# VectorE's side stages moved from the end of a step to the middle of it, in a graph-attention kernel on one core

## The chip, the cores and the metric

The kernel runs on 1 core of a Trainium2 chip. The metric is the time of the kernel on the device in microseconds (us), here the median of 3 runs. Engines: TensorE (PE in the profile) multiplies matrices, VectorE (DVE), ScalarE (ACT) and GpSimd (POOL) work elementwise, SyncE (SP) starts DMAs. Each engine has one queue of instructions, taken in order, and they wait for each other on semaphores.

## The reference, cut to what matters

x has 4096 rows of 128 numbers, adj is 4096 by 4096; there are 8 heads of 16.

```python
qkv = layer_norm(x, g1, be1) @ w_qkv
q, k, v = ...                                       # 8 heads of 16
scores = jnp.einsum('nhd,mhd->hnm', q, k) * SCALE
scores = jnp.where((adj != 0)[None, :, :], scores, -jnp.inf)
attn = jax.nn.softmax(scores, axis=-1)
out = jnp.einsum('hnm,mhd->nhd', attn, v).reshape(n, DIM)
x = x + out @ w_proj + b_proj
h2 = layer_norm(x, g2, be2)
return x + jax.nn.gelu(h2 @ w1 + b1) @ w2 + b2
```

## The kernel before

**Tiles and steps.** After a first stage (keys, values, the first masks) the queries are worked off in 8 tiles of 512 rows, i = 0 to 7; a short last pass, i = 8, finishes tile 7. Each tile has STEPS = 64 steps g: 4 pairs of heads, 16 steps for each. A step has two blocks n = 0 and 1 of 128 keys. `made_by(i)` gives three flags: b (there is a next tile), c (a tile is being made), d (there is a tile before, whose output is being finished).

**What TensorE does in a step** (`body`, from line 941): `scores(g, 0)`; a stage for ScalarE if there is one (`act_fill`); `weigh_values` of step g - 3 (L879, probabilities times values); `scores(g, 1)`; a stage for VectorE if there is one (`dve_fill`). `scores` holds the two score matmuls of the block (L964, L966), in banks of 4 that ScalarE empties with exp (L614, two exps a step), and after each of them one `row` (L815). Two matmuls (L976) add the mask; where `pool_masked` holds, in block 1 of the odd steps g for the most part (28 of the 64 steps), they are left out, and GpSimd masks the probabilities instead. Such a block is called whole below.

**The rows.** They run ahead, for the next pair of heads or tile: each of a step's UNITS = 4 rows is a 128 by 512 tile of scores of which VectorE takes the masked maximum (`row_maximum`, L652). r0 and r1 stand in block 0, r2 and r3 in block 1. Row tiles and VectorE's side stages go through one ring of three PSUM banks, `ring_ps`. The order in it is written out by hand: `ROW_PLACE` and `DVE_PLACE` number its places, and TensorE writes a place only when VectorE has taken all up to the one three places before (`place - 3`). A place that a tile doesn't use (tile 0 has no stages for a tile before) still counts as a place.

**VectorE's side stages** (`DVE_FILLS`, line 71): "sums" at steps 4, 20, 36, 52 (TensorE L912, then a reciprocal L749), "back" at steps 5, 21, 37, 53 (L918, then a multiplication L752), "proj" at step 7 (L925, then an addition L756 and the layer norm's statistics L298 to L306), "down" at steps 23 and 25 (L935 and L937, then an addition L763). The sums and back of steps 20 to 53 belong to the tile being made (flag c), all others to the tile before (flag d).

**ScalarE's side stages** (`ACT_FILLS`, line 67) stand after block 0; "shift" is at steps 4, 20, 36 and 52 among others, "q" at 24, 27, 33, 40. After step 21 ScalarE makes the gelu (L620), whose result "down" reads; after step 9 it makes a square root (L625) for which VectorE waits at step 10.

Of the kernel before, what the change touches and what calls it, by code (L numbers as in the profile page):

```python
# [25 lines left out]
CHUNKS = N // 512  # L26
# [31 lines left out]
UNITS = 4  # L58
# [12 lines left out]
DVE_FILLS = {4: ("sums", PAIRS - 1), 5: ("back", PAIRS - 1), 7: ("proj",), 23: ("down", 0), 25: ("down", 1)}  # L71
# [30 lines left out]
def fills_of(table, b, c, d):  # L102
    on = {"b": b, "c": c, "d": d}
    return {g: w for g, w in table.items() if on[made_for(w)]}
# [3 lines left out]
SCORE_PLACE, ACT_PLACE, ROW_PLACE, DVE_PLACE = {}, {}, {}, {}  # L108
for _g in range(STEPS):
    for _b in range(BLOCKS):  # L110
        SCORE_PLACE[_g, _b] = len(SCORE_PLACE) + len(ACT_PLACE)
        if _b == 0 and _g in ACT_FILLS:
            ACT_PLACE[_g] = len(SCORE_PLACE) + len(ACT_PLACE)
    for _x in range(UNITS):
        ROW_PLACE[_g, _x] = len(ROW_PLACE) + len(DVE_PLACE)
    if _g in DVE_FILLS:
        DVE_PLACE[_g] = len(ROW_PLACE) + len(DVE_PLACE)
SCORE_PLACES = len(SCORE_PLACE) + len(ACT_PLACE)
ROW_PLACES = len(ROW_PLACE) + len(DVE_PLACE)
assert SCORE_PLACES % 2 == 0 and ROW_PLACES % 3 == 0 and FIRST_UNITS % 3 == 0  # L120
# [2 lines left out]
def row_steps(b, c):  # L123
    return STEPS if b else (STEPS - AHEAD if c else 0)
# [35 lines left out]
def pool_masked(p, m):  # L160

    return m % 4 == 3 and not (p == 2 and m % 8 == 7)
# [22 lines left out]
def row_unit(g, x):  # L185

    u = UNITS * (g + AHEAD) + x
    ahead, u = divmod(u, TILE_UNITS)
    p, u = divmod(u, QUARTER_UNITS)
    j, u = divmod(u, 2 * CHUNKS)  # L190
    return ahead, p, j, u // 2, 1 - u % 2
# [7 lines left out]
def program(nc, x, adj, w_qkv, w_proj, b_proj, w1, b1, w2, b2, g1, be1, g2, be2, const, out):  # L199
    with ExitStack() as ctx:  # L200
# [115 lines left out]
        def neg_max_order(i, p, jj):  # L316

            return i * (PAIRS * 2) + (p * 2 + jj)

        def made(ring, i, bcd, place):  # L320

            return ring.before(i) + ring.upto(bcd, place)
# [313 lines left out]
        def _(dve):  # L636
# [20 lines left out]
            def negated_maxima(n, jj, taken):  # L657

                if not (isinstance(n, int) and n < 2):
                    dve.wait_ge(split_step, SPLIT_OPS * (n - 1))  # L660
                dve.wait_ge(row_taken, taken)
                nc.vector.tensor_reduce(neg_max[:, jj, :], row_max[:, 2 * jj:2 * jj + 2, :, :], AX.X, ALU.max,  # L662
                                        negate=True).then_inc(neg_max_done, 1)
# [51 lines left out]
            for st in range(FIRST_STEPS):  # L715
# [7 lines left out]
                if st >= ROW_LAG:  # L723
                    ch, j = divmod(st - ROW_LAG, SUB)
# [11 lines left out]
            for g in range(-LEAD, 0):  # L736
                for x in range(UNITS):
                    _, p, j, ch, a = row_unit(g, x)
# [4 lines left out]
            def take_fill(i, par, bcd, g, what):  # L743

                bank = ring_ps[:, DVE_PLACE[g] % 3, :]
                full = made(ROWS, i, bcd, DVE_PLACE[g])
                dve.wait_ge(row_full, full)
                if what[0] == "sums":
                    nc.vector.reciprocal(recip[:, :, :], bank[:, 0:2 * SUB].rearrange("p (s a) -> p s a", a=2))\  # L749
                      .then_inc(row_taken, 1)  # L750
                elif what[0] == "back":
                    nc.vector.tensor_tensor(attn[:, what[1], :], bank, attn[:, what[1], :], ALU.mult)\  # L752
                      .then_inc(row_taken, 1)
                elif what[0] == "proj":
                    dve.wait_ge(x_res_in, i * 16)
                    nc.vector.tensor_tensor(x_res[:, :, :].rearrange("p s d -> p (s d)"), bank,  # L756
                                            x_res[:, :, :].rearrange("p s d -> p (s d)"), ALU.add)\
                      .then_inc(row_taken, 1)
                    dve.wait_ge(row_taken, full)
                    layer_norm_stats(lambda k: dve.wait_ge(ln2_step, (i - 1) * LN_STEPS + k), ln2_step, x_res)  # L760
                elif what[0] == "down":
                    s = 2 * what[1]
                    nc.vector.tensor_tensor(rows2[:, s:s + 2, :].rearrange("p s d -> p (s d)"), bank[:, 0:256],  # L763
                                            x_res[:, s:s + 2, :].rearrange("p s d -> p (s d)"), ALU.add)\
                      .then_inc(row_taken, 1)

            def body(i, par, b, c, d):
                bcd = b, c, d
                fills = fills_of(DVE_FILLS, b, c, d)
                for g in range(STEPS):  # L770
                    if d and g == APPLY_STEP:
                        dve.wait_ge(rstd_done, TILES + i)
                        layer_norm_apply(ln2_step, x_res, rows2)
                    if g < row_steps(b, c):
                        for x in range(UNITS):
                            ahead, p, j, ch, a = row_unit(g, x)
                            if p == 0 and ch % 2 == 0 and a == 1:
                                dve.wait_ge(mask_done, (i + ahead) * CONVERTED + (j * ADJ_C + ch // 2 + 1))
                            taken = made(ROWS, i, bcd, ROW_PLACE[g, x])
                            dve.wait_ge(row_full, taken)  # L780
                            row_maximum(ROW_PLACE[g, x], j, a, ch)
                        if j % 2 == 1 and ch == CHUNKS - 1:
                            negated_maxima(neg_max_order(i + ahead, p, j // 2), j // 2, taken)
                    if g in fills:
                        take_fill(i, par, bcd, g, fills[g])

            run_iterations(body)

# [1 line left out]
        def _(pe):  # L790
# [38 lines left out]
            for st in range(FIRST_STEPS):  # L829
                blk, p = st // PAIRS, st % PAIRS  # L830
# [9 lines left out]
                if st >= ROW_LAG:  # L840
                    ch, j = divmod(st - ROW_LAG, SUB)
# [7 lines left out]
            for g in range(-LEAD, 0):  # L849
                for x in range(UNITS):  # L850
                    _, p, j, ch, a = row_unit(g, x)
# [89 lines left out]
            def body(i, par, b, c, d):  # L941
                bcd = b, c, d
                act_fills, dve_fills = fills_of(ACT_FILLS, b, c, d), fills_of(DVE_FILLS, b, c, d)

                def row(g, x):
                    if g >= row_steps(b, c):
                        return
                    ahead, p, j, ch, a = row_unit(g, x)
                    place = ROW_PLACE[g, x]
                    pe.wait_ge(row_taken, made(ROWS, i, bcd, place - 3))  # L950
                    row_scores(q_stack[par if ahead == 0 else 1 - par], place, j, p, a, ch)

                def scores(g, n):

                    p, m = g // QUARTER, BLOCKS * (g % QUARTER) + n
                    place = SCORE_PLACE[g, n]
                    half = 2 * (place % 2)
                    even, odd = score_ps[:, half, :], score_ps[:, half + 1, :]
                    whole = pool_masked(p, m)
                    keys = k_stack[:, p, 128 * m:128 * (m + 1)]  # L960
                    low, high = slice(0, KROWS), slice(HALF, HALF + KROWS)
                    score_turn(i, bcd, place)
                    settled(pe)
                    nc.tensor.matmul(even, keys[low, :], q_stack[par][low, p, :], start=True, stop=whole)  # L964
                    row(g, 2 * n)
                    last = nc.tensor.matmul(odd, keys[high, :], q_stack[par][high, p, :], start=True, stop=whole)  # L966
                    if whole:
                        last.then_inc(score_full, 1)
                    row(g, 2 * n + 1)
                    if whole:  # L970
                        return
                    if p == 0 and m % PER_C == 0:
                        pe.wait_ge(mask_in[m // PER_C], (i + 1) * (16 * SUB))
                        settled(pe)
                    for bank in (even, odd):
                        last = nc.tensor.matmul(bank, ident_bf[:, :], mask_t[:, m, :], start=False, stop=True)  # L976
                    last.then_inc(score_full, 1)

                for g in range(STEPS):
                    for n in range(BLOCKS):  # L980
                        if c:
                            scores(g, n)
                        if n == 0 and g in act_fills:
                            act_fill(i, bcd, g, act_fills[g])
                        if n == 0 and g < LAG and d:
                            weigh_values(i - 1, made_by(i - 1), STEPS - LAG + g)
                        if n == 0 and g >= LAG and c:
                            weigh_values(i, bcd, g - LAG)
                    if g in dve_fills:
                        dve_fill(i, bcd, g, dve_fills[g])  # L990

            run_iterations(body)

# [32 lines left out]
```

## Time and profile before

| what | value |
|---|---|
| median of 3 runs | 2086.73 us (2084.29 to 2088.51) |
| the profiled execution's own time | 2088.21 us |
| its span, first to last instruction | 2085.9 us |
| TensorE busy | 1892.9 us (91%), granted clock 0.966 on average |
| VectorE, ScalarE, GpSimd busy | 1433.2 (69%), 1370.7 (66%), 1120.8 us (54%) |
| tiles 0 to 7, first step to first step | 222.5, 245.1, 243.6, 245.0, 245.4, 244.2, 244.1 us; tile 7 starts at 1805.3 |

A row of the page or of a view of the trace is read so: times are us from the span's start, L964 is line 964 of the kernel, "<-" stands between what is written and what is read, and the bracket at the end of a row is the idle time of the engine ahead of it and who ended it. A matmul's duration is longer than its place in the stream, since matmuls overlap; so the starts of L964 are used as marks, and a distance between two of them is the time that the work between them takes.

### The profile page before, as it was taken

Reading aid. Unit: us, or ns where it says so; the run is one execution under the profiler, and the core shown is the slowest. Engines: PE = TensorE matmul, PEld = TensorE weight load, DVE = VectorE, ACT = ScalarE, POOL = GpSimd, SP = SyncE. Lnnn points to the kernel's source line nnn. Section 1 sums busy time; section 2 is a strip of 40 time slices with the busy share of each in tenths; the row PEclk is TensorE's granted clock in tenths of the full one; section 3 lists DMA queues with packets and bytes.
Section 4 is the critical chain, followed back from the end, with each engine's and each line's share of the span. In section 5 each row is a group of like instructions: output and inputs, shape, how many; then the busy total and the mean of one; then the engine's idle time right before and its main releaser. Section 6 shows DMA issues by size and latency. Waiting matters only on the chain.

```text
span 2085.9 us, 37539 instructions
## 1 busy us (share of the span) xinstructions
PE 1892.9 (91%) x12226; PEld 530.0 (25%) x12226; DVE 1433.2 (69%) x4495; ACT 1370.7 (66%) x1431; POOL 1120.8 (54%) x1026
## 2 busy tenths in 40 slices
PE   6899999899999999899998999989998999989996
PEld 2212222232222222222222322222222222222224
DVE  6987777667776677667776677766777577766600
ACT  5656766666666666566666667667666667666681
POOL 5744675447654566446754476445754467543340
PEclk9889999999999999999999999999999999999995
DMA  8600234003420035001440024200341014300000
GB/s 213 148 6 1 67 101 87 1 6 100 97 58 1 26 117 98 19 1 57 116 87 1 6 81 107 67 1 26 107 88 40 1 57 116 68 1 6 1 1 10
DMA packets 168662, 114.50 MB, mean 55 GB/s; under 512 B 139283, under 2 KB 149014, under 8 KB 168470
## 3 DMA queue, kind: packets, MB, share of 16 engines
q1 hardware_dynamic: 157718, 103.71, 20.6%
q10 hardware_dynamic: 10752, 8.39, 1.3%
q8 instruction: 100, 1.64, 0.3%
q14 instruction: 92, 0.75, 0.1%
HBM read 74.33 MB, written 4.19 MB: 38 GB/s over the span
## 4 chain that ended last, share of the span: by engine, by line
PE 71%; ACT 11%; issue 9%; DVE 5%; POOL 2%; DMA 1%; DVEq 0%; SPq 0%; POOLq 0%; ACTq 0%
PE pv_ps L879 20%; PE score_ps L976 17%; PE score_ps L964 11%; ACT probs L614 9%; PE ring_ps L815 9%; PE score_ps L966 2%; PE ring_ps L935 2%; PE score_ps L902 2%; DVE masked_out L652 2%; PE ring_ps L925 2%; PE score_ps L892 1%; PE score_ps L838 1%; PE ring_ps L912 1%; PE ring_ps L918 1%; DVE row_max L652 1%
## 5 line engine op out<-in xcount | busy, mean ns | idle before, releaser
L652 DVE CUSTOM_DVE_ANT_0 masked_out<-ring_ps,row_mask 128x512 bf16<-128x512 f32 x2048 | 1303.9, 687 | 467.9 <-PE ring_ps L815 463.9
L614 ACT ACTIVATE probs<-score_ps,score_scale 128x1024 f32<-128x1024 f32 x1024 | 1139.3, 1115 | 616.6 <-PE score_ps L976 492.4
L815 PE MATMUL ring_ps<-k_stack,q_stack 51*128 51x512 f16 x2048 | 646.9, 391 | 88.4 <-DVE row_max L652 87.6
L471 POOL TENSOR_SCALAR probs<-probs 128x1024 f32<-128x1024 f32 x224 | 233.3, 1042 | 702.6 <-ACT probs L614 702.1
L879 PE MATMUL pv_ps<-probs,v_ones 128*17 128x512 f32 x4096 | 552.5, 607 | 20.0 <-ACT attn L587 17.0
L477 POOL TENSOR_TENSOR probs<-probs,keep 128x1024 f32<-128x1024 f32 x224 | 476.9, 2129 | 40.3 <-POOL probs L471 29.6
L976 PE MATMUL score_ps<-mask_t,ident_bf 128*128 128x512 bf16 x1600 | 490.6, 389 | 0.0
L964 PE MATMUL score_ps<-q_stack,k_stack 51*128 51x512 f16 x1024 | 396.7, 388 | 41.8 <-ACT probs L614 41.1
L966 PE MATMUL score_ps<-q_stack,k_stack 51*128 51x512 f16 x1024 | 389.1, 380 | 0.0
L964 PEld LDWEIGHTS score_ps<-q_stack,k_stack 51*128 51x128 f16 x1024 | 95.2, 93 | 650.9 <-issue 642.0
L815 PEld LDWEIGHTS ring_ps<-k_stack,q_stack 51*128 51x128 f16 x2048 | 147.7, 94 | 261.4 <-DVE row_max L652 207.3
L652 DVE DVE_READ_ACCUMULATOR2_ANT row_max<- 128x1 f32 x2048 | 169.1, 83 | 0.0
L976 PEld LDWEIGHTS score_ps<-mask_t,ident_bf 128*128 128x128 bf16 x1600 | 91.1, 97 | 248.2 <-issue 248.2
L416 POOL TENSOR_SCALAR row_mask<-row_mask 128x1024 bf16<-128x1024 bf16 x124 | 130.0, 1048 | 24.1 <-POOL row_mask L412 24.1
L412 POOL TENSOR_SCALAR row_mask<-adj_in 128x1024 bf16<-128x1024 uint32 x124 | 129.1, 1041 | 8.9 <-DMA adj_in<-adj 2.9
L879 PEld LDWEIGHTS pv_ps<-probs,v_ones 128*17 128x17 f32 x4096 | 73.1, 96 | 228.7 <-issue 167.2
L966 PEld LDWEIGHTS score_ps<-q_stack,k_stack 51*128 51x128 f16 x1024 | 98.1, 96 | 7.3 <-issue 0.8
L510 ACT COPY q_stack<-score_ps 2x256 f16<-2x256 f16 x128 | 46.6, 364 | 9.5 <-PE score_ps L795 7.2
L749 DVE RECIPROCAL recip<-ring_ps 128x8 f32<-128x8 f32 x32 | 6.6, 207 | 64.6 <-PE ring_ps L912 62.3
L902 PE MATMUL score_ps<-h2T,w_sb 128*128 128x512 f32 x64 | 39.8, 707 | 7.4 <-ACT hidden L579 2.3
L493 POOL TENSOR_TENSOR q_stack<-q_x,q_neg 128x512 f16<-128x512 f32 x28 | 32.4, 1157 | 25.8 <-ACT q_x L572 25.8
L421 POOL TENSOR_SCALAR max_unit<-neg_max 128x4 f32<-128x4 f32 x64 | 12.7, 199 | 59.4 <-DVE neg_max L662 31.3
(89 smaller groups left out, 911.8 us busy)
## 6 DMA issues: line engine op xcount, KB each, us to landing
adj_in<-adj SPq DMA_DIRECT2D x128, 512.0 KB, 4.1
xnT_dram<-attn ACTq DMA_DIRECT2D x8, 256.0 KB, 4.1
mask_t<-row_mask SPq DMA_TRANSPOSE x128, 3.3
xq<-xnT_dram ACTq DMA_DIRECT2D x8, 256.0 KB, 4.5
x_res<-x ACTq DMA_DIRECT2D x8, 256.0 KB, 3.0
out<-rows ACTq DMA_DIRECT2D x8, 256.0 KB, 2.3
w_sb<-L_gnn_w SPq DMA_DIRECT2D x2, 256.0 KB
probs<-x SPq DMA_DIRECT2D x1, 256.0 KB, 2.9
```

The costliest lines, as they stand in the source:

```text
L412: nc.gpsimd.tensor_scalar(target, adj_in[:, half, :].bitcast(U32), 1.0, 0.0, ALU.min, ALU.max)\
L416: nc.gpsimd.tensor_scalar(target, target, BIG, -BIG, ALU.mult, ALU.add).then_inc(mask_done, 1)
L471: nc.gpsimd.tensor_scalar(flat, flat, 128.0, 0.0, ALU.min, ALU.max).then_inc(probs_bounded, 1)
L477: nc.gpsimd.tensor_tensor(view, view, keep[:, m // 4, :].unsqueeze(1).broadcast_to([128, 2, TILE]), ALU.mult).then_inc(probs_masked, 1)
L614: nc.scalar.activation(probs[:, (2 * g + n) % SLOTS, :], score_ps[:, half:half + 2, :].rearrange("p a n -> p (a n)"), ACT.Exp, scale=score ...
L652: nc.vector.tensor_tensor_reduce(out=masked_out[:, place % 3, :], in0=ring_ps[:, place % 3, :], in1=row_mask[:, j, ch * 512:(ch + 1) * 512 ...
L815: nc.tensor.matmul(ring_ps[:, place % 3, :], stack[rows, p, 128 * j:128 * (j + 1)], k_stack[rows, p, ch * 512:(ch + 1) * 512], start=True, ...
L879: last = nc.tensor.matmul(pv_ps[32 * k:32 * k + HD + 1, :], v_ones[:, BLOCKS * (g % QUARTER) + b, 2 * p + a, :], probs[:, (2 * g + b) % SL ...
L902: last = nc.tensor.matmul(bank, w1_sb[:, 128 * f:128 * (f + 1)], h2T[:, :], start=True, stop=True)
L964: nc.tensor.matmul(even, keys[low, :], q_stack[par][low, p, :], start=True, stop=whole)
L966: last = nc.tensor.matmul(odd, keys[high, :], q_stack[par][high, p, :], start=True, stop=whole)
L976: last = nc.tensor.matmul(bank, ident_bf[:, :], mask_t[:, m, :], start=False, stop=True)
```

## The change: where the stages of VectorE stand

In TensorE's program `dve_fill` moves from the end of the step to between `act_fill` and `weigh_values`, that is between the step's first block and its values. VectorE takes it after r1 in place of after r3, and the ring's places are numbered so. The negated maxima stay at the step's end; none of them is in a step with a side stage. No instruction is added or removed.

```diff
@@ -113,8 +113,8 @@
             ACT_PLACE[_g] = len(SCORE_PLACE) + len(ACT_PLACE)
     for _x in range(UNITS):
         ROW_PLACE[_g, _x] = len(ROW_PLACE) + len(DVE_PLACE)
-    if _g in DVE_FILLS:
-        DVE_PLACE[_g] = len(ROW_PLACE) + len(DVE_PLACE)
+        if _x == UNITS // 2 - 1 and _g in DVE_FILLS:
+            DVE_PLACE[_g] = len(ROW_PLACE) + len(DVE_PLACE)
@@ -771,18 +771,18 @@
-                    if g < row_steps(b, c):
-                        for x in range(UNITS):
+                    for x in range(UNITS):
+                        if g < row_steps(b, c):
                             ahead, p, j, ch, a = row_unit(g, x)
                             if p == 0 and ch % 2 == 0 and a == 1:
                                 dve.wait_ge(mask_done, (i + ahead) * CONVERTED + (j * ADJ_C + ch // 2 + 1))
                             taken = made(ROWS, i, bcd, ROW_PLACE[g, x])
                             dve.wait_ge(row_full, taken)
                             row_maximum(ROW_PLACE[g, x], j, a, ch)
-                        if j % 2 == 1 and ch == CHUNKS - 1:
-                            negated_maxima(neg_max_order(i + ahead, p, j // 2), j // 2, taken)
-                    if g in fills:
-                        take_fill(i, par, bcd, g, fills[g])
+                        if x == UNITS // 2 - 1 and g in fills:
+                            take_fill(i, par, bcd, g, fills[g])
+                    if g < row_steps(b, c) and j % 2 == 1 and ch == CHUNKS - 1:
+                        negated_maxima(neg_max_order(i + ahead, p, j // 2), j // 2, taken)
@@ -982,12 +982,12 @@
                             scores(g, n)
                         if n == 0 and g in act_fills:
                             act_fill(i, bcd, g, act_fills[g])
+                        if n == 0 and g in dve_fills:
+                            dve_fill(i, bcd, g, dve_fills[g])
                         if n == 0 and g < LAG and d:
                             weigh_values(i - 1, made_by(i - 1), STEPS - LAG + g)
                         if n == 0 and g >= LAG and c:
                             weigh_values(i, bcd, g - LAG)
-                    if g in dve_fills:
-                        dve_fill(i, bcd, g, dve_fills[g])
```

## Rows read from the trace of the kernel before

**Rows 1.** Waits of TensorE in tile 1 (366 to 611): total, times, longest.

```profile
PE ring_ps L815 <- DVE row_max L652: 10.0, 23, 3.1
```

**Rows 2.** Timeline, TensorE and VectorE, ordinary blocks of tile 1: start, duration.

```profile
362.46 0.39 PE L964 MATMUL score_ps<-q_stack,k_stack 51*128 51x512 f16 x1
363.54 0.39 PE L964 MATMUL score_ps<-q_stack,k_stack 51*128 51x512 f16 x1
365.64 0.39 PE L964 MATMUL score_ps<-q_stack,k_stack 51*128 51x512 f16 x1
...
376.40 0.39 PE L964 MATMUL score_ps<-q_stack,k_stack 51*128 51x512 f16 x1
376.84 0.38 PE L964 MATMUL score_ps<-q_stack,k_stack 51*128 51x512 f16 x1
376.98 0.69 DVE L652 CUSTOM_DVE_ANT_0 masked_out<-ring_ps,row_mask 128x512 bf16<-128x512 f32 x1 [0.65 <-PE ring_ps L815]
377.74 0.39 PE L815 MATMUL ring_ps<-k_stack,q_stack 51*128 51x512 f16 x1 [0.29 <-DVE row_max L652]
379.57 0.39 PE L964 MATMUL score_ps<-q_stack,k_stack 51*128 51x512 f16 x1
```

**Rows 3.** Timeline of TensorE, step 4 of tile 1, with its sums.

```profile
351.56 0.38 PE L964 MATMUL score_ps<-q_stack,k_stack 51*128 51x512 f16 x1
354.74 0.37 PE L964 MATMUL score_ps<-q_stack,k_stack 51*128 51x512 f16 x1 [0.29 <-ACT probs L614]
355.73 0.95 PE L912 MATMUL ring_ps<-sum_sel,attn 128*128 128x2 f32 x8
356.61 0.39 PE L964 MATMUL score_ps<-q_stack,k_stack 51*128 51x512 f16 x1
```

**Rows 4.** Timeline of TensorE, step 5 of tile 1, with its back.

```profile
358.67 0.39 PE L964 MATMUL score_ps<-q_stack,k_stack 51*128 51x512 f16 x1
359.20 1.08 PE L918 MATMUL ring_ps<-ident,recip 128*32 128x128 f32 x32
360.21 0.39 PE L964 MATMUL score_ps<-q_stack,k_stack 51*128 51x512 f16 x1
```

**Rows 5.** Timeline of TensorE and VectorE after the proj of tile 1.

```profile
369.94 0.39 PE L964 MATMUL score_ps<-q_stack,k_stack 51*128 51x512 f16 x1
372.58 0.69 DVE L652 CUSTOM_DVE_ANT_0 masked_out<-ring_ps,row_mask 128x512 bf16<-128x512 f32 x1
373.33 0.39 PE L815 MATMUL ring_ps<-k_stack,q_stack 51*128 51x512 f16 x1 [0.72 <-DVE row_max L652]
```

**Rows 6.** Timeline of TensorE and ScalarE around the gelu of tile 1.

```profile
428.06 0.39 PE L964 MATMUL score_ps<-q_stack,k_stack 51*128 51x512 f16 x1
431.19 1.91 ACT L620 ACTIVATE hidden<-hidden 128x2048 f32<-128x2048 f32 x1
435.67 0.37 PE L964 MATMUL score_ps<-q_stack,k_stack 51*128 51x512 f16 x1 [2.68 <-ACT probs L614]
```

**Rows 7.** Timeline of TensorE, step 25 of tile 1, with its down.

```profile
448.95 0.39 PE L964 MATMUL score_ps<-q_stack,k_stack 51*128 51x512 f16 x1
449.49 1.16 PE L935 MATMUL ring_ps<-w_sb,hidden 128*128 128x128 f32 x8
...
452.49 0.39 PE L964 MATMUL score_ps<-q_stack,k_stack 51*128 51x512 f16 x1
454.55 0.39 PE L964 MATMUL score_ps<-q_stack,k_stack 51*128 51x512 f16 x1
```

**Rows 8.** Timeline of TensorE, step 6 of tile 0.

```profile
134.61 0.38 PE L964 MATMUL score_ps<-q_stack,k_stack 51*128 51x512 f16 x1
137.96 0.39 PE L964 MATMUL score_ps<-q_stack,k_stack 51*128 51x512 f16 x1
```

**Rows 9.** Busy time by stretches, behind two gelus; granted clock after the five engines.

```profile
436.00:441.00 5.00, 5.00 (x27) 1.98 (x23) 2.62 (x8) 2.76 (x3) 0.25 (x1) 0.66 0.00 0
681.00:686.00 5.00, 5.00 (x37) 2.61 (x33) 2.62 (x8) 2.89 (x3) 1.04 (x1) 1.00 0.02 3
```

## The prediction, made before the changed kernel was run

> **What bounds the kernel now.** I read the table of busy times first: TensorE is the busiest engine by far, and no other reaches three quarters of the span. Since the change adds no instruction, its work stays, and only its pauses can change. So I took the waits next [rows 1], where the reader should see that a tile has 23 pauses of TensorE for VectorE, most of them small, and then the timeline of one tile. I marked every start of L964, two in a step: T0 is the time from a step's block 0 to its block 1, T1 the time from block 1 to the next step. These times repeat from tile to tile to within a few hundredths of a us, save in the places named below, so one tile can be summed.
>
> **The ring's ordinary loss.** Behind an even step T1 is 363.54 - 362.46 = 1.08, and T0 of the odd step 365.64 - 363.54 = 2.10 [rows 2]. An odd step's block 1 is mostly whole: T1 is 376.84 - 376.40 = 0.44. Then the four rows r2, r3 and the next step's r0, r1 come in one burst, r1 may be written only when r2 has been taken, and VectorE starts r2 0.58 after the mark (376.98). TensorE issues r1 at 377.74, 1.34 after the mark, and T0 is 379.57 - 376.84 = 2.73. Free of such a loss T0 is 454.55 - 452.49 = 2.06 [rows 7]. So a burst costs 2.74 - 2.06 = 0.68 behind a whole block (the bracket's 0.29 is what is left of it beside matmuls still ending), and 0.04 behind a masked one. A side stage at the end of an odd step stands in the middle of this burst and covers the loss. After the change it stands ahead of the values instead, where VectorE has caught up anyway, and the burst is whole again. That is the heart of my forecast.
>
> **What a stage costs TensorE.** At the end of a whole block it starts 359.20 - 358.67 = 0.53 after the mark, at the place where the next block would have started at 0.44: its price is its length F + 0.09. Behind a masked block it is cheaper: for the sums, F = 356.61 - 355.73 = 0.88 [rows 3], T1 = 356.61 - 354.74 = 1.87 against 1.08, so 0.79 = F - 0.09. Block 0 is always masked, so I price the new place at F - 0.08. F is 360.21 - 359.20 = 1.01 for a back [rows 4], 452.49 - 449.49 = 3.00 for a down [rows 7], and 4.30 - 0.53 = 3.77 for the proj, from 369.94 - 365.64 [rows 2, 5]. No row shows matmuls of a back followed by the values; between F - 0.17 and F + 0.09 I take F - 0.08.
>
> **Sums at 4, 20, 52** (even steps). T0 is now 354.74 - 351.56 = 3.18 [rows 3]: 2.74 and 0.44 more, since block 1 waits for ScalarE's exp of block 0, as the shift between them takes a place in its ring. With the sums ahead of block 1, that wait is covered: T0 = 2.74 + 0.79 = 3.53, T1 = 1.08, together 4.61 against 3.18 + 1.87 = 5.05. **-0.44 each.** At step 36 TensorE waits ahead of the shift, for GpSimd, and nothing is gained: +0.01.
>
> **Back at 5, 37, 53** (odd steps). Before: 358.67 - 356.61 = 2.06, then 1.54, then 362.46 - 360.21 = 2.25, sum 5.85 [rows 2 to 4]. After: 2.10 + 0.93, then 0.44, then 2.74, sum 6.21. **+0.36 each.**
>
> **Back at 21.** Here ScalarE sets the pace: exp of block 1, a table load, the gelu of 1.91, a table load, exp of step 22, and TensorE may start step 23. From mark to mark that is 435.67 - 428.06 = 7.61, with 2.68 of idle TensorE [rows 6]. Nothing in this chain moves. The back stands inside the stretch now and costs nothing; after the change it stands ahead of it, while the stretch stays 7.61. Cost 2.10 + 0.93 + 7.61 against 2.06 + 7.61: **+0.97.** The idle part grows to some 2.68 + 1.55 + 2.25 - 0.44 - 2.74 = 3.3.
>
> **Proj at 7.** VectorE's chain of addition and statistics ends 372.58 - 369.94 = 2.64 after the matmuls, and the row that waits is issued at 373.33, 3.39 after them [rows 5]. Before, that was r3 of step 8; from 369.94 to 376.40 are 6.46. After, block 1 of step 7 starts 0.98 behind the proj, is whole, step 8 starts at 1.42, and its r1 waits for r2 of step 7, which queues behind the chain: it too goes out at 3.39, where 1.64 was its turn. The loss is 1.75, and block 1 of step 9 follows (the values take 2.06 - 1.08 = 0.98) after 0.98 + 0.44 + 2.06 + 1.75 + 1.08 + 2.10 = 8.41. Before, from the masks of step 7: 0.53 + 0.98 + 4.30 + 6.46 = 12.27; after: 0.45 + 3.77 + 8.41 = 12.63. **+0.36.** Behind VectorE's chain nothing but rows is queued. ScalarE's square root follows its exps of step 9 and is no earlier for earlier statistics.
>
> **Down at 23 and 25.** Before 2.10 + 3.54 + 2.06 = 7.70 [rows 7]; after 2.10 + 2.92 + 0.44 + 2.74 = 8.20. **+0.50 each.** The gelu is done by then: TensorE gets past block 0 of step 23 only behind an exp that follows it.
>
> **Tiles 1 to 6:** 3 x -0.44 + 0.01 + 3 x 0.36 + 0.97 + 0.36 + 1.00 = +2.10 each, 12.6 in all.
>
> **Tile 0** has no stages for a tile before, but their places count. At a step's end such an empty place leaves the burst two banks in place of three: T0 of step 6 is 137.96 - 134.61 = 3.35 [rows 8], 0.61 above 2.74. There are five (behind 4, 5, 7, 23, 25). In the new place the missing bank falls beside the values, where no row waits. So 5 x -0.61 = -3.05, with 2 x -0.44 + 0.01 + 3 x 0.36 = +0.21: -2.8.
>
> **Tile 7** has no rows after step 42 and no q stages; steps 52 and 53 lose their part, the empty q place of step 24 already holds block 1 back. I take +0.7, between 0 and 2.1. The last pass has no rows and nothing to cross: 0.
>
> **Clock.** Behind the gelu's pause TensorE goes on at the granted clock 1.00 in some tiles and at a mean of 0.66 in others, in part at 1.2 in place of 2.4 GHz [rows 9]: four tiles of seven (1, 3, 4, 6). In tile 1, from the mark behind the gelu to block 1 of step 25, are 448.95 - 435.67 = 13.28 [rows 6, 7]; the same marks in a tile with no drop are 2.06 + 3.54 + 2.92 + 1.08 + 2.10 = 11.70 apart, so a drop costs 1.58. The pause grows from 2.7 to 3.3 us; at step 10, where it is 3.1 [rows 1], the clock drops in all seven tiles. I take six of seven: 2 x 1.58 = +3.1, between -3 and +5. The Trainium skill (TensorE: Matmul & The Clock Gate, "HAM oscillation — how this bites in real kernels") says that waits of TensorE which come again in each round can put it at half clock in each round. This trace agrees for the gelu's wait, in four tiles of seven.
>
> **Sum.** 12.6 - 2.8 + 0.7 + 3.1 = +13.6. On the profiled execution's 2088.2 (span 2085.9 and 2.3 around it) that is 2101.8; it lies 1.5 above the median of the runs, so against 2086.7 I forecast 2100.3 us.
>
> **Rivals.**
> (a) **The burst's loss doesn't come back** (faster). If VectorE, rid of the stage, took r2 in time, the 0.68 would fall away behind steps 5, 37, 53, 23 and 25: 3.4 per tile, 20.4 in tiles 1 to 6, 2.0 in tile 0, 2.3 in tile 7. 13.6 - 24.7 = -11, 2076 us. It decides if r1 can go out 0.66 after the mark, where it goes out at 1.34. Against it: each whole block without a stage shows the loss, with VectorE idle for 0.65 ahead of r2 [rows 2], so it isn't lateness of VectorE but one row's passage. 5%.
> (b) **The order is neutral.** If the waits only changed places and TensorE met each of them once: 2087 us. Speaks for it that -0.44 and +0.36 nearly cancel for each sums and back; against it the gelu and the downs. 7%.
> (c) **The clock reacts harder.** If all seven gelus are followed by a drop, and one twice as long, as behind step 10, this is 10 x 1.58 = 15.8 in place of 3.1: 2113 us. By the page's rule the longer wait speaks for it. 12%.
> (d) The forecast's mechanism, with 2092 to 2107: 76%.
>
> **How the numbers follow.** The likeliest is (d), 2100.3. The bounds of the unknown costs: the clock -6 and +2, the stages' new place (some 55 stages, 0.09 either way) 5, tile 7 1; taken together 8 below, 6 above. The range 2092 to 2109 leaves out (a), (b) and most of (c), some 2 in 10. About 0.2% (4 us) is what a measurement of this kernel can tell from no change. Faster by more: 0.05; within: 0.08; slower: 0.87.
>
> **What the new profile would show.** T0 of steps 6, 26, 38 and 54 at 2.74; of step 4 near 3.53 with no bracket of ScalarE; the gelu's idle at 3.3; the wait for VectorE at step 8 on r1, with 1.4 idle; T0 of step 6 in tile 0 at 2.74. I am wrong if T0 behind the moved stages stays near 2.1, if the gelu's pause doesn't grow, or if GpSimd's masked probabilities, used three steps later, become late where they aren't now.

## The result and the profile after

The changed kernel takes 2125.1 us (median; 2121.7 to 2128.7) against 2087.6 for the kernel before on the same chip: +37.5 us, a ratio of 1.0179, 95% interval 1.0151 to 1.0208. The forecast was 2100.3, with a range of 2092 to 2109. The direction was right, the size wrong by a factor of 2.8.

The page of the changed kernel, its first lines, the granted clock by slices and three groups of section 5:

```profile
span 2126.4 us, 37539 instructions
...
PE 1917.5 (90%) x12226; PEld 548.5 (26%) x12226; DVE 1432.7 (67%) x4495; ACT 1370.8 (64%) x1431; POOL 1120.8 (53%) x1026
...
PEclk9889999999999999999999899998999899999996
...
L815 PE MATMUL ring_ps<-k_stack,q_stack 51*128 51x512 f16 x2048 | 644.7, 392 | 106.4 <-DVE row_max L652 105.8
...
L879 PE MATMUL pv_ps<-probs,v_ones 128*17 128x512 f32 x4096 | 551.2, 608 | 20.0 <-ACT attn L587 17.0
...
L964 PE MATMUL score_ps<-q_stack,k_stack 51*128 51x512 f16 x1024 | 398.0, 389 | 39.3 <-ACT probs L614 38.7
```

The same instructions keep TensorE busy for 1917.5 us in place of 1892.9, 24.6 more, while its idle time in the span grows by 15.9 (from 193.0 to 208.9). So the larger part of the loss is one that no wait shows. A lower clock is one source of it. Matmuls that ran beside others and now stand alone are another, at an unchanged clock: in the run with the sums alone, below, TensorE is busy for 1904.5 us at a mean clock of 0.967. TensorE's wait for VectorE ahead of the rows is 105.8 where it was 87.6. The mean granted clock is 0.957 against 0.966.

The marks (starts of L964) match the prediction's at most places. The table gives the growth of T0 + T1, in us, for a tile in which no drop of the clock falls into the steps:

| stage | predicted | measured |
|---|---|---|
| sums at 4, 20, 52 | -0.44 | -0.04 |
| sums at 36 | +0.01 | +0.33 |
| back at 5, 37, 53, with the next step | +0.36 | +0.32 |
| back at 21, to the gelu's end | +0.97 | +0.93 |
| proj at 7, steps 7 to 9 | +0.36 | +0.24 (0.28 and 0.48 in two tiles) |
| down at 25, with the next step | +0.50 | +0.38 |
| tile 0's five empty places, each | -0.61 | -0.61 |

The burst is back whole. Timeline of TensorE around step 5 of tile 1, which answers to [rows 4] and [rows 2]:

```profile
356.74 0.39 PE L964 MATMUL score_ps<-q_stack,k_stack 51*128 51x512 f16 x1
...
357.86 1.08 PE L918 MATMUL ring_ps<-ident,recip 128*32 128x128 f32 x32
358.75 1.04 PE L879 MATMUL pv_ps<-probs,v_ones 128*17 128x512 f32 x8
359.73 0.39 PE L964 MATMUL score_ps<-q_stack,k_stack 51*128 51x512 f16 x1
...
360.17 0.38 PE L964 MATMUL score_ps<-q_stack,k_stack 51*128 51x512 f16 x1
...
361.07 0.39 PE L815 MATMUL ring_ps<-k_stack,q_stack 51*128 51x512 f16 x1 [0.30 <-DVE row_max L652]
```

The back stands ahead of the values, block 1 is whole (0.44), and r1 of step 6 goes out 361.07 - 359.73 = 1.34 behind the mark, exactly the delay of an ordinary burst.

The pause for the gelu, to be read against [rows 6], and the stretch behind one of them (tile 4), by time and by busy shares (the number after the five engines is the granted clock):

```profile
428.63 0.39 PE L964 MATMUL score_ps<-q_stack,k_stack 51*128 51x512 f16 x1
...
429.07 0.38 PE L964 MATMUL score_ps<-q_stack,k_stack 51*128 51x512 f16 x1
...
436.24 0.37 PE L964 MATMUL score_ps<-q_stack,k_stack 51*128 51x512 f16 x1 [3.29 <-ACT probs L614]
```

```profile
1184.00:1194.00 10.00, 9.43 (x38) 5.41 (x40) 1.73 (x5) 2.54 (x3) 0.00 (x0) 0.50 0.00 0
```

From 428.63 to 436.24 are 7.61, as before, and the idle part is 3.29, as predicted. But behind the gelu of tile 4 the clock is at the lower of its levels (1.2 GHz) for 10 us, where [rows 9] has 0.66 over 5. From the mark behind the gelu to block 0 of step 25 a tile of this order takes 9.98 without a drop (9.57 in tile 7, which has no q stage), as the runs below show where no drop comes; the seven tiles took 11.55, 14.15, 11.55, 15.51, 15.33, 15.23 and 12.69. That is 26.6 us lost to the clock, against 6.3 in the kernel before (four drops, to the same mark, where 9.60 is the time without one); I had written 9.4.

### The profile page after: what moved, and what is told of

Its sections match the earlier page's. It is cut to its first block, busy times and chain, and to the rows that moved or that the text cites. A ratio compares the mean times of both kernels' runs of the same rounds, so it can differ in the third digit from the quotient of the medians.

```text
span 2126.4 us, 37539 instructions
## 1 busy us (share of the span) xinstructions
PE 1917.5 (90%) x12226; PEld 548.5 (26%) x12226; DVE 1432.7 (67%) x4495; ACT 1370.8 (64%) x1431; POOL 1120.8 (53%) x1026
## 4 chain that ended last, share of the span: by engine, by line
PE 71%; issue 10%; ACT 10%; DVE 5%; POOL 2%; DMA 1%; DVEq 0%; SPq 0%; POOLq 0%; ACTq 0%
PE pv_ps L879 20%; PE score_ps L976 17%; PE score_ps L964 11%; PE ring_ps L815 8%; ACT probs L614 8%; PE ring_ps L935 2%; PE score_ps L966 2%; DVE masked_out L652 2%; PE score_ps L902 2%; PE ring_ps L918 2%; PE ring_ps L912 2%; PE score_ps L892 1%; PE ring_ps L925 1%; PE score_ps L838 1%; DVE row_max L652 1%
## 5 line engine op out<-in xcount | busy, mean ns | idle before, releaser
L815 PE MATMUL ring_ps<-k_stack,q_stack 51*128 51x512 f16 x2048 | 644.7, 392 | 106.4 <-DVE row_max L652 105.8
L879 PE MATMUL pv_ps<-probs,v_ones 128*17 128x512 f32 x4096 | 551.2, 608 | 20.0 <-ACT attn L587 17.0
L964 PE MATMUL score_ps<-q_stack,k_stack 51*128 51x512 f16 x1024 | 398.0, 389 | 39.3 <-ACT probs L614 38.7
L964 PEld LDWEIGHTS score_ps<-q_stack,k_stack 51*128 51x128 f16 x1024 | 95.4, 93 | 660.3 <-issue 648.8
L879 PEld LDWEIGHTS pv_ps<-probs,v_ones 128*17 128x17 f32 x4096 | 74.0, 96 | 210.8 <-issue 154.7
L763 DVE TENSOR_TENSOR rows<-ring_ps,x_res 128x256 f32<-128x256 f32 x16 | 6.8, 425 | 71.0 <-PE ring_ps L937 71.0
L935 PE MATMUL ring_ps<-w_sb,hidden 128*128 128x128 f32 x256 | 49.6, 356 | 1.4 <-ACT hidden L579 0.9
L935 PEld LDWEIGHTS ring_ps<-w_sb,hidden 128*128 128x128 f32 x256 | 45.2, 259 | 9.4 <-issue 5.7
```

Of the source, the lines that this page charges most:

```text
L815: nc.tensor.matmul(ring_ps[:, place % 3, :], stack[rows, p, 128 * j:128 * (j + 1)], k_stack[rows, p, ch * 512:(ch + 1) * 512], start=True, ...
L879: last = nc.tensor.matmul(pv_ps[32 * k:32 * k + HD + 1, :], v_ones[:, BLOCKS * (g % QUARTER) + b, 2 * p + a, :], probs[:, (2 * g + b) % SL ...
L935: nc.tensor.matmul(bank[:, 128 * s:128 * (s + 1)], hidden[:, f, 128 * t:128 * (t + 1)], w2_sb[:, f, :], start=(f == 0), stop=False)
```

## The experiments

All but the pair without the gelu are built alike: a set MIDDLE names the steps whose side stage stands in the middle, all others stand at the step's end as before; where a run moves something else besides, its own edit follows. Every kernel was also set against the kernel before on its chip (medians 2089.3, 2090.5, 2090.9 in the three series).

```diff
+MIDDLE = {...}
@@ places, VectorE and TensorE alike @@
-    if _g in DVE_FILLS:
-        DVE_PLACE[_g] = len(ROW_PLACE) + len(DVE_PLACE)
+        if _x == (1 if _g in MIDDLE else UNITS - 1) and _g in DVE_FILLS:
+            DVE_PLACE[_g] = len(ROW_PLACE) + len(DVE_PLACE)
...
+                        if n == 0 and g in dve_fills and g in MIDDLE:
+                            dve_fill(i, bcd, g, dve_fills[g])
...
-                    if g in dve_fills:
+                    if g in dve_fills and g not in MIDDLE:
                         dve_fill(i, bcd, g, dve_fills[g])
```

**Sums alone.** First behind the shift, as in the change, then ahead of it.

```diff
+MIDDLE = {4, 20, 36, 52}
```

> Only the sums of steps 4, 20, 36 and 52 stand in the middle of their step, behind ScalarE's shift; all other side stages stay at the step's end. Theory A (the sums lose cover there: the shift's four small transposes, which now run beside the values, and the sums' first weight load are exposed): time from block 0 to block 1 of step 4 stays 3.92 as in the changed kernel, sum of the terms 22 x -0.05 + 8 x 0.33, less 0.6 for tile 0, about +1 us against the kernel before; up to +5 if the clock drops behind some of them. Rival (the 0.39 comes from a neighbour's stage, the back of the next step being in the middle too): 3.53, and 22 x -0.44 - 0.6, about -10 us.

Measured: 2094.8 us, ratio 1.0033 (1.0019 to 1.0047). T0 of step 4 is 3.93 again, that of step 36 3.84. So the loss doesn't come from a neighbour's stage. In three places (steps 4 of tiles 2 and 3, step 52 of tile 6) T0 + T1 is 1.6 longer still: a drop of the clock behind sums, with no pause longer than 0.7 us in the steps ahead of it.

```diff
+MIDDLE = {4, 20, 36, 52}
...
+                        if n == 0 and g in dve_fills and g in MIDDLE:
+                            dve_fill(i, bcd, g, dve_fills[g])
                         if n == 0 and g in act_fills:
                             act_fill(i, bcd, g, act_fills[g])
-                        if n == 0 and g in dve_fills and g in MIDDLE:
-                            dve_fill(i, bcd, g, dve_fills[g])
```

> As the run with the sums alone in the middle, but ahead of ScalarE's shift, so that the shift again stands beside the values. Theory A (the shift hides beside the values and its weight loads run ahead there): time from block 0 to block 1 of step 4 is 3.53 to 3.6, against 3.92 behind the shift, and the kernel is 8 to 10 us faster than before. Rival (the exposed part is the sums' own, wherever they stand in block 0's neighbourhood): 3.9 again, +1 us.

Measured: 2073.4 us, ratio 0.9924 (0.9906 to 0.9941), 15.8 us faster, more than the 8 to 10 expected. T0 of step 4 is 3.61, and at step 36 the wait for GpSimd ahead of the shift is covered as well: T0 is 2.97 with the sums in it, where it was 2.74 without them, which the expectation had not counted: 4.2 us in eight tiles by the marks. Timelines of TensorE in step 4 of tile 1, first of the changed kernel, then of this one (L795 and L798 are the shift, L912 and L915 the sums, L879 and L882 the values):

```profile
352.95 0.60 PE L976 MATMUL score_ps<-mask_t,ident_bf 128*128 128x512 bf16 x2
...
353.49 0.28 PE L795 MATMUL score_ps<-ident_h,max_part 128*2 128x128 f16 x4
...
353.69 1.05 PE L912 MATMUL ring_ps<-sum_sel,attn 128*128 128x2 f32 x8
...
354.68 1.05 PE L879 MATMUL pv_ps<-probs,v_ones 128*17 128x512 f32 x8
...
355.66 0.39 PE L964 MATMUL score_ps<-q_stack,k_stack 51*128 51x512 f16 x1
```

```profile
353.40 0.60 PE L979 MATMUL score_ps<-mask_t,ident_bf 128*128 128x512 bf16 x2
...
353.84 0.95 PE L915 MATMUL ring_ps<-sum_sel,attn 128*128 128x2 f32 x8
...
354.72 0.22 PE L798 MATMUL score_ps<-ident_h,max_part 128*2 128x128 f16 x2
...
354.74 0.62 PE L882 MATMUL pv_ps<-probs,v_ones 128*17 128x512 f32 x2
...
355.79 0.39 PE L967 MATMUL score_ps<-q_stack,k_stack 51*128 51x512 f16 x1
```

The reader should see two gaps in the first and none in the second. Behind the masks the shift starts after 0.54 and the sums 0.20 later, and they take 0.99 to the values; together 1.73. Ahead of the shift the sums start 0.44 behind the masks, take 0.88, and the shift costs 0.02, since it runs side by side with the values: 1.34. The 0.39 between them is what I had missed; 0.32 of it is left at the next mark (T0 3.61 against 3.93), as the values beside the shift take 0.07 longer.

**The back of step 21 and the down of step 23**, alone and together.

```diff
+MIDDLE = {21}
```

> Only the back of step 21 stands in the middle; TensorE's pause for the gelu grows from 2.7 to 3.3 us, and what follows it is as before (values and a dense block ahead of the down at step 23's end). +0.93 per tile in tiles 1 to 7, +0.3 in tile 0: +6.8 us without the clock. Theory P (the length of the pause sets the clock): all seven gelus are followed by a drop and some by a long one of 3 to 4 us, +15 to +25 us in all. Theory D (what TensorE does behind the pause sets it): drops stay at about 1.6 us each, +7 to +12 us.

Measured: 2101.3 us, ratio 1.0058 (1.0039 to 1.0076). T0 of step 21 is 2.94, the pause 3.29. The clock drops behind all seven gelus, six times for 1.6 us and once for 2.6: 11.9 us lost. The kernel before had four drops of seven, but the run with the sums alone had seven at the old pause of 2.68, so this run doesn't show that the longer pause brings more of them. It does show that the longer pause alone brings no drops of 4 us.

```diff
+MIDDLE = {23}
```

> Only the down of step 23 stands in the middle, 1 us behind the gelu's pause of 2.7 us, which stays as it is. Without the clock +0.4 per tile and -0.6 in tile 0: +2 us. Theory P (the length of the pause sets the clock): drops as before the change, in about four tiles of seven and of 1.6 us, +2 to +4 us in all. Theory D (the down's short matmuls behind the pause keep the clock low): step 23 costs 3 to 4.3 us more than 5.4 in the tiles where the clock falls, +8 to +20 us in all.

Measured: 2098.6 us, ratio 1.0045 (1.0029 to 1.0060). The pause is 2.68, yet all seven gelus are followed by a drop, and five of them are long: 3.1, 3.1, 1.6, 4.2, 1.6, 3.1 and 3.1 us, 19.9 in all. (The drops at step 10 hide a part of it in the total; see the list of terms below.) The down at half clock in tile 1, to be read against [rows 7]:

```profile
434.95 0.37 PE L967 MATMUL score_ps<-q_stack,k_stack 51*128 51x512 f16 x1 [2.68 <-ACT probs L615]
...
436.09 1.91 PE L938 MATMUL ring_ps<-w_sb,hidden 128*128 128x128 f32 x8
437.94 0.79 PE L940 MATMUL ring_ps<-b_row,ones_row 1*128 1x128 f32 x2
438.66 2.08 PE L938 MATMUL ring_ps<-w_sb,hidden 128*128 128x128 f32 x8
```

```diff
+MIDDLE = {21, 23}
```

> Two moves together: the back of step 21 (the pause for the gelu grows to 3.3 us) and the down of step 23 (short matmuls 1 us behind the pause) stand in the middle, all else at the step's end. Alone they gave +12 and +9 us. If they are independent: +21 us. Theory PD (the long pause and the short matmuls feed one low stretch of the clock, longer than either makes): step 23 and block 0 of step 24 lose 3 to 4.4 us to the clock in each of seven tiles, as in the changed kernel, +28 to +33 us against before.

Measured: 2100.7 us, ratio 1.0047 (1.0031 to 1.0062). Theory PD falls, and so does the sum of the two single moves. All seven gelus are followed by a drop, but each costs 1.4 to 1.6 us, 10.8 in all: +10.3 us on the median, where the single moves gave 12.0 and 9.3. So neither the pause nor the down behind it sets the length by itself, and neither do the two together, since the changed kernel has both and drops of up to 5.5.

**The changed kernel with one thing undone.**

```diff
+MIDDLE = {4, 5, 7, 20, 21, 23, 25, 36, 37, 52, 53}
@@ against the changed kernel, TensorE's program @@
-                        if n == 0 and g in dve_fills:
+                        if n == 0 and g in dve_fills and g in MIDDLE and g not in (23,):
                             dve_fill(i, bcd, g, dve_fills[g])
...
                             weigh_values(i, bcd, g - LAG)
+                        if n == 0 and g in dve_fills and g in MIDDLE and g in (23,):
+                            dve_fill(i, bcd, g, dve_fills[g])
```

> The changed kernel, with one edit in TensorE's program alone: at step 23 the down's matmuls stand behind the values in place of ahead of them. Places of the ring, pause and all work are the changed kernel's. Theory D (what TensorE runs first behind the pause decides how long the clock stays low): the values come first, the drop is shorter by 1 to 2 us per tile, 2110 to 2118 us. Theory P (only the pause of 3.3 us matters): 2125 as the changed kernel.

```diff
+MIDDLE = {4, 5, 7, 20, 21, 25, 36, 37, 52, 53}
```

> The changed kernel with only the down of step 23 back at the step's end. Without the clock -0.4 per tile, +0.6 in tile 0, 2 us less than the changed kernel. Theory D: block 1 and the values stand between pause and down again, the gelu's drops cost 1.6 us in all seven tiles as with the back of step 21 alone: 2105 to 2110 us. Theory P: the drops keep their 3 to 4 us, 2121 to 2124 us.

Measured: 2116.4 us, ratio 1.0125 (1.0104 to 1.0146), and 2117.4 us, ratio 1.0127 (1.0101 to 1.0153). The gelus' drops cost 19.5 and 15.7 us in the two traces, against 26.6 in the changed kernel. The first is inside what theory D had named (2110 to 2118), the second between the two theories. Moving the down away shortens the drops, without bringing them back to 1.6 each (with the down at the step's end they were 1.6, 2.6, 1.6, 2.9, 1.6, 2.9 and 2.7). Each list is of one execution.

**The gelu taken away.**

```diff
                         nc.scalar.activation(hidden[:, :, :].rearrange("p f n -> p (f n)"),
                                              hidden[:, :, :].rearrange("p f n -> p (f n)"),
-                                             ACT.Gelu_apprx_tanh).then_inc(gelu_done, 1)
+                                             ACT.Identity).then_inc(gelu_done, 1)
```

> The kernel before with the gelu that ScalarE makes after step 21 replaced by a copy, in all tiles but the last pass: the work of one function is left out, and with it its two table loads of 1.3 us. TensorE's pause of 2.7 us in seven tiles should be gone, and with it the clock's drop behind it: 7 x 2.7 + 6 = 25 us faster than before, some 2063 us. It is the partner of the next run.

> The changed kernel with the same gelu replaced by a copy. The difference to its partner is what the change costs apart from the gelu. Theory G (the back of step 21 loses its cover and the clock falls for longer behind the pause; this is most of the 37 us): from the marks of the other steps the difference is +14 us, up to +19 with the clock's drops behind the sums. Rival (the clock is lower in the changed kernel because of the ring's small waits all over, whatever the gelu): the difference stays above +30 us.

Measured: 2062.5 us, ratio to the kernel before 0.9866 (0.9844 to 0.9887), and 2078.9 us, ratio 0.9949 (0.9928 to 0.9969). Without the gelu the change costs 16.5 us in place of 37.5, inside the 14 to 19 expected: theory G holds. The copy leaves no pause at that place in the first kernel and one of 0.44 in the second. No drop follows step 21 in either (9.64 and 9.98 from mark to mark in every tile from 1 to 6), although the ring's waits are all there, as the first waits of the second kernel show, and the mean clock is the same in both (0.973 and 0.974):

```profile
PE ring_ps L815 <- DVE row_max L652: 107.5, 236, 3.1
PE score_ps L964 <- ACT probs L614: 19.0, 63, 0.7
```

**The rest alone.**

```diff
+MIDDLE = {5, 7, 25, 37, 53}
```

> Only the stages of steps 5, 7, 25, 37 and 53 stand in the middle, no sums and nothing near the gelu. From the terms: back +0.32 to +0.36 at 5, 37, 53, proj +0.24 to +0.36, down of 25 +0.39 to +0.50 per tile, tile 0 less 0.6 behind steps 5, 7, 25: +9 us with the prediction's terms, +8 with those of the changed kernel's marks. Rival (a) of the prediction (the rows' burst costs nothing once the stage is gone from it): -8 us.

Measured: 2098.2 us, ratio 1.0041 (1.0027 to 1.0056), +7.3 us. Rival (a) is out. By the marks the backs cost 5.2 us in all tiles, the proj 1.3, the down of step 25 2.1, with tile 0's gains in them; in the trace drops behind the gelus add 3.1 to these 8.6, and steps 10 to 12 take 6.9 less.

**A kernel that beats both.** TensorE's pause for the gelu is free time. The back of step 21 stood in that stretch already; now it stands one step later in it, the sums of step 20 go in as well, and the other sums stand ahead of the shift.

```diff
+DVE_FILLS[21], DVE_FILLS[22] = DVE_FILLS.pop(20), DVE_FILLS.pop(21)
+MIDDLE = {4, 36, 52}
```

> A candidate for better than both. The sums of steps 4, 36 and 52 stand in the middle ahead of ScalarE's shift; the sums of step 20 move to the end of step 21 and the back of step 21 to the end of step 22, both into TensorE's pause for the gelu; all else as before. From the marks: -0.36 at steps 4 and 52, -0.55 at 36, -0.79 for the sums that the pause hides, in tiles 1 to 7, and -0.6 for tile 0's empty place: about -16 us; the pause shrinks from 2.7 to 1.7 us, so the gelu's clock drops should vanish (another -6): 2065 to 2070 us. If the stretch from step 21 to 23 is longer than ScalarE's chain once both stages are in it: no gain from the sums of step 20, 2073 us.

Measured: 2067.6 us, ratio 0.9887 (0.9862 to 0.9912), 22.8 us faster than the kernel before. Timeline of TensorE and ScalarE through the pause of tile 1 (L916 are the sums, L922 the back), and the stretch behind it:

```profile
433.57 0.39 PE L968 MATMUL score_ps<-q_stack,k_stack 51*128 51x512 f16 x1
...
434.11 1.05 PE L916 MATMUL ring_ps<-sum_sel,attn 128*128 128x2 f32 x8
...
436.70 1.91 ACT L622 ACTIVATE hidden<-hidden 128x2048 f32<-128x2048 f32 x1
...
438.44 1.08 PE L922 MATMUL ring_ps<-ident,recip 128*32 128x128 f32 x32
...
441.18 0.37 PE L968 MATMUL score_ps<-q_stack,k_stack 51*128 51x512 f16 x1 [1.66 <-ACT probs L616]
```

```profile
441.00:447.00 6.00, 5.66 (x39) 3.14 (x42) 2.74 (x9) 3.27 (x4) 1.56 (x2) 1.00 0.00 0
```

From 433.57 to 441.18 are 7.61 once more, the pause is 1.66, and the clock stays at 1.00 behind all seven gelus. By the marks the sums give 12.0 + 4.2 us (steps 4, 20, 52 and step 36), the missing drops 6.3 and steps 10 to 12 3.1. This trace's span is still only 17.4 below that of the kernel before, as its first stage, which no edit touches, took 6.9 longer, with the clock at 0.50 from 108.8 us to the first step at 122.4.

```diff
+MIDDLE = {4, 23, 36, 52}
```

> The candidate with the sums of step 20 and the back of step 21 in the gelu's pause, and the down of step 23 in the middle besides. The pause is 1.7 us. Theory P+ (a pause of 2.7 us or more starts the drop, the down's short matmuls behind it only lengthen it): no drop, +0.4 per tile, -0.6 in tile 0: +2 us against the candidate, 2070 us. Theory D alone (the short matmuls near the pause start it): the clock falls as in the run with the down alone, +12 to +20 us against the candidate, 2080 to 2088 us.

Measured: 2071.9 us, ratio to the kernel before 0.9919 (0.9893 to 0.9945). No drop behind any gelu: 9.98 from mark to mark against 9.60, the down's plain 0.38. It is 4.3 us slower than the kernel beside it, where 2 was expected and 12 to 20 by theory D; the two intervals overlap. The same move that cost 13.6 us of clock at a pause of 2.7 costs none at 1.7.

## Why the prediction was wrong, step by step

The direction and most terms held. Two terms of the sum failed, the price of the sums' new place and the clock's drops behind the gelu.

- **What bounds the kernel.** TensorE does, but the sentence that its work stays and only its pauses can change was wrong: 24.6 of the 40.5 us between the two spans are busy time. The two terms that failed, the sums and the clock, are of this kind.
- **The ring's loss.** Right: a whole block followed by rows costs 0.68 (T0 of steps 6, 26, 38 and 54 is 2.74). The proj, the downs of step 25, the back of step 21 and tile 0's empty places came out within 0.12 us of their terms.
- **Sums at 4, 20, 52 and 36.** The mechanism was right, ScalarE's wait is covered; the price of the new place was wrong. I took F - 0.08 from the sums behind masks, and forgot that the shift stands between the masks and the new place. Behind the masks it ran beside the values at no cost; ahead of the sums it stands alone, and the sums' first weight load starts with their first matmul, where it starts 0.15 ahead of it when the sums come first. -0.44 became -0.04, +0.01 became +0.33: 0.40 three times and 0.32 once a tile, about 11 us in all (22 x 0.40 and 7 x 0.32; tile 7 differs). The two runs with the sums alone settle it: 15.8 us faster one way round, 5.5 slower the other.
- **Clock.** The term that failed most: +3.1 predicted, 26.6 - 6.3 = +20.3 in the trace. Its frequency was nearly right (seven of seven, six predicted), its length was not: I priced each drop at 1.58, as in the one trace that I had, while they cost 1.6 to 5.5. Rival (c) had the longer drops, at 12%. Its words and its sum don't agree: seven drops with one of them twice as long cost 4 x 1.58 more than the four there were, and 10 x 1.58 is what all seven twice as long would add. Even that is below the 20.3 measured. The range's upper bound gave the clock 2 us above my value, which contradicts the rival beside it. A bound was to be had from rows: a stretch of 9.6 us behind the gelu at half clock all through would lose as much again, and the worst tiles lost a little over half of that.
- **Drops elsewhere.** Not in the sum at all. Three fall in steps with sums in the changed kernel (+4.7). At step 10 all seven tiles have one in both kernels, but they are shorter (-4.0). That is no gain of the change: in all the other traces, too, steps 10 to 12 take 1.0 to 6.9 us less than in the trace of the kernel before. Its step 10 was at the dear end, and a ledger against this one trace carries that.
- **Rival (a)** and **(b)** are refuted by the run with the rest alone and by the pair without the gelu.

The changed kernel's 40.5 us between the two spans, from the marks: sums 3.1 (drops among them) and 2.5, backs 5.4, proj 1.3, step 21 and 22 6.8, steps 23 and 24 22.4, down of step 25 2.1, steps 10 to 12 -4.0, the rest, with the first stage and the last pass, 0.9. The traced execution of the changed kernel is 3 us above its median, so the medians are only 37.5 apart. In this total the shorter drops of step 10, which nobody had forecast, stand against the missed terms and hide 4.0 us of them; that is luck.

**How long a drop behind the gelu lasts.** The drops cost 1.5 us each in the run with both moves, 3 in that with the down alone and up to 5.5 in the changed kernel. The traces order them by where the clock falls, against the mark at which TensorE starts again. Tile 4 of the changed kernel, whose mark is at 1184.52 (granted clock after the five engines):

```profile
1183.90:1184.00 0.10, 0.00 (x0) 0.00 (x0) 0.00 (x0) 0.10 (x1) 0.00 (x0) 1.00 0.00 0
1184.10:1197.60 13.50, 13.03 (x46) 6.52 (x46) 4.27 (x13) 4.43 (x5) 1.48 (x2) 0.50 0.01 1
```

The clock falls at 1184.0, 0.52 ahead of the mark, while TensorE still waits. Over nine kernels the cost of one drop in us is:

| the clock falls | down ahead of the values (3 kernels) | down at the step's end (6 kernels) |
|---|---|---|
| 0.5 to 1.1 us ahead of the mark | 5.2 to 5.5 (3 drops) | 2.6 to 2.9 (5 drops) |
| 0.35 ahead to 0.65 behind | 1.4 to 1.6 (11) | 1.5 to 1.6 (18) |
| 0.65 to 1.55 behind | 3.1 to 4.2 (7) | 1.5 to 1.6 (13) |

All seven drops of the run with both moves are in the middle row; five of the seven with the down alone are in the last, and the three dearest of the changed kernel in the first. So the down ahead of the values makes a drop dearer only where the clock falls early or late. This is an order found in the traces, not one that a run was made to show. (With the down behind the values three drops that begin 0.7 to 1.1 ahead cost 2.8 to 3.0, but one that begins 0.48 ahead cost 5.7.)

**What stays open.** What decides where the clock falls. The Trainium skill (TensorE: Matmul & The Clock Gate, "What's actually happening") says, of the start of a kernel, that the number of slow matmuls differs from run to run of one kernel. The changed kernel's executions differ in this way too, though its drops are not at the start: its spans were 2120.0 twice and 2126.4 and 2126.9, at mean clocks of 0.961 and 0.957. Whether the time between two gelus (242.8 to 245.4 us in the kernel before, 248.3 to 253.0 in the changed one) plays a part was not tried.

## What to carry to other kernels

Before a stage is moved, look what it covers where it stands (here a burst of rows, and a table load's pause) and what it pulls apart where it goes (here small transposes that ran beside the values). A pause of TensorE that another engine sets is the one place where its work is free; moving work out of it costs the work and lengthens the pause, moving work in pays twice. Where the clock already drops in some rounds, price a change near that place with a range, not with the mean of one trace.

## What the runs showed of the hardware

- Four transposes of 2 columns (the shift) cost TensorE 0.02 us ahead of the values' narrow matmuls (17 columns of weights) and 0.20 ahead of matmuls with 128 by 128 weights.
- Behind a pause of 1.66 us the clock never fell (14 gelus in two kernels); behind 2.68 it fell in 29 of 35 (five kernels); behind 3.29 in all 35 (five kernels). These kernels differ in the work around the pause too, not in its length alone. The clock can fall with no pause over 0.7 us in the steps ahead, where the sums' matmuls of 2 columns stand behind the shift: T0 + T1 of a step is 1.6 longer in three of 31 places, in the changed kernel as in that with the sums alone, and in 11 of 155 over the five kernels with this order. With the sums ahead of the shift or at the step's end no trace has such a fall.
- A stage of fp32 matmuls costs less between masks and values than its length: the down 2.81 for 3.00, the back 0.89 for 1.01.
